# Query-part stores ahead of the heads' traffic, DVE's wait for them at the first context write, maxima turned two units later

## The chip, the cores and the metric

One core of a Trainium2 chip runs the whole program. The metric is the device time of one execution in microseconds (us); lower is better. The engines are PE (TensorE, matrix products), DVE (VectorE), ACT (ScalarE), POOL (GpSimd) and SP (SyncE, which here only issues DMAs).

## The reference

Two adaptive-layernorm blocks over x of 1024 tokens by 512, all float32. The first holds grouped-query attention with rotary embedding and a small feed-forward part, the second a mixer and a gated feed-forward part. What matters here is the attention of the first block:

```python
q = (x @ Wq.T).reshape(b, t, H, DH).transpose(0, 2, 1, 3)      # H = 32, DH = 16
k = (x @ Wk.T).reshape(b, t, HKV, DH).transpose(0, 2, 1, 3)    # HKV = 8, so 4 query heads for each
q = q * cos + _rotate_half(q) * sin
scores = jnp.einsum('bhgtd,bhkd->bhgtk', qg, k) / math.sqrt(DH)
scores = jnp.where(causal, scores, finfo.min)
attn = jax.nn.softmax(scores, axis=-1)
ctx = jnp.einsum('bhgtk,bhkd->bhgtd', attn, v)
```

and the modulation rows `mod = silu(c) @ wmod` of both blocks, most of which are computed in the shade of the attention.

## The kernel before

**Queries in three parts.** Queries and keys are split into three bf16 parts, whose products give float32 accuracy. The first quarter of the queries is split by DVE. The other three are done by POOL in `rope_queries(c)`, c = 1 to 3: seven operations over 128 x 1024 that end in the tile `qparts` and raise `part_q`. SP stores `qparts` to the scratch `q_parts` in DRAM (semaphore `q_out`), from where `load_queries` and `load_keys` bring the rows of each head into the stacks `Qst` and `Kst`. There is one `qparts`, so `rope_queries(c)` first waits for store c - 1 to land. The tiles `qacc`, `qraw` and `qsw` that POOL works in share their memory with `att`, into which DVE writes the contexts; so DVE must see `part_q >= 3` before its first context write.

**POOL's order** is `rope_queries(1)`, `head_v(0)`, `weigh(0)`, `rope_queries(2)`, `weigh(1)`, `rope_queries(3)`, `head_v(1)`, `weigh(2)`, and so on. `weigh(h)` multiplies a piece of the modulation weights `wmr` (1.28 MB, loaded by SP) and sums it into `wsum`.

**A head body.** There are eight key-value heads. `head_body(n)` interleaves three heads. Head n goes through 36 transposed units (`t_unit`: PE scores of 128 keys x 512, ACT exp into `pr`) and nine PV rounds of PE. Head n + 1 gets the rest of its 20 score units (`s_unit`: PE products into bank pair 0/1 or 2/3, DVE maximum over the row into `mxp`), and head n + 2 its first six. A PE score unit waits until DVE has read the unit two slots before it. After head n + 1's last score unit come its maxima: DVE forms `nm`, PE transposes it (`max_turn`, L937), DVE makes three bf16 parts of it (`maxima`, L1699 to L1704), and SP writes them as rows 96 to 98 of `Qst` (`head_dmas`, L736), which `t_unit(n + 1, 0)` needs. PE's `mod_step` is the product of the piece in `wsum`, which DVE copies to `full` (L1708). The maxima use bank 0 and the mod product bank 2, each as one slot in the same order of slots. `ctx_turn` and `ctx_norm` finish head n - 1 in body n, after score unit 7.

The function `body_steps` lays out the order: each piece has a cost, and its step is the transposed unit behind which PE issues it. PE issues pieces in the list's order once the unit count has reached their step; DVE follows the same list without steps. In bodies 1 to 5 the maxima stand behind unit 24, the mod product behind unit 26, the next head's first score unit behind unit 27 and its second behind unit 28. In body 0 maxima and mod stand behind units 23 and 25, in body 6 behind 25 and 27.

**SP's order.** SP issues its DMAs strictly in program order and stops at each wait. After the loads for heads 0 and 1 it goes through `head_dmas(h)` (waits for the maxima of head h, then the row DMAs, the modulation row, and the next `wmr`), then store h + 1 while h < 3, then the loads for head h + 2, which from h = 1 on wait for all of body h - 1's units.

Of the kernel before, what the change touches and what calls it, by code (L numbers as in the profile page):

```python
# [291 lines left out]
def reduce_cost(s):  # L292

    i, _, heads, kh = SUNITS[s]
    return 160 + heads * width(i, kh)
# [14 lines left out]
def ctx_at(n):  # L310

    if n >= NKV - 2:
        return slots_before(NKV) + 2 * (n - (NKV - 2))
    return slots_before(n + 2, "ctx")
# [6 lines left out]
def body_steps(nxt, nxt2, ctx):  # L321


    todo = []
    if nxt:
        for s in range(AHEAD, NS):
            if s == CTX_AT and ctx:
                todo.append(("ctx", -1, None, 1400))
            todo.append(("s", 1, s, reduce_cost(s)))
        todo.append(("max", 1, None, 1600))  # L330
        todo.append(("mod", 1, None, 300))
    elif ctx:
        todo.append(("ctx", -1, None, 1400))
    if nxt2:
        todo += [("s", 2, s, reduce_cost(s)) for s in range(AHEAD)]
    total = sum(x[3] for x in todo)
    out, sofar = [], 0
    for what, d, s, cost in todo:
        step = sofar * NTU // max(total, 24000)
        out.append((max(step, 3) if what == "ctx" else step, what, d, s))  # L340
        sofar += cost
    return out

# [38 lines left out]
def adaln_two_blocks(nc, a, out):  # L382
    banks, pieces, prods = plan()
    with ExitStack() as ctx:
        cursor = [MISC_B]

        def at(name, shape, dt, offset=None):

            if offset is None:
                offset = cursor[0]  # L390
                size = 4 if dt in (F32, F32R) else 2
                for n in shape[1:]:
                    size *= n
                cursor[0] += (size + 31) // 32 * 32
            return nc.alloc_sbuf_tensor_at(name, shape, dt, offset=offset)

        def sem(name):
            return ctx.enter_context(nc.semaphore(name))
# [41 lines left out]
        qparts = at("qparts", [P, 3, T], BF16, WR_B + 40 * 1024)  # L440
# [94 lines left out]
        qscr = nc.dram_tensor("q_parts", (NKV // 2, 3, P, T), BF16, kind="Internal").ap()  # L535
# [23 lines left out]
        q_raw, part_q = sem("later_queries_copied"), sem("later_query_parts_ready")  # L559
        sw_done = sem("later_queries_swapped")  # L560
        kst_ones = sem("key_rows_of_ones_ready")
        q_out = sem("later_query_parts_out")
# [73 lines left out]
        class Chain:  # L636
# [5 lines left out]
            def link(self, ins):  # L642
                ins.then_inc(self.s, 1)
                self.n += 1
                if self.turn is None:
                    self.eng.wait_ge(self.s, self.n)
                else:
                    self.eng.wait_ge(self.s, self.turn * self.per + self.n)
# [18 lines left out]
        Q_ROWS = ((0, 3), (1, 2), (2, 1))  # L667
        K_ROWS = (3, 2, 1)
        assert sum(n for _, n in Q_ROWS) == sum(K_ROWS) == 6

        block = ctx.enter_context(nc.Block())
# [3 lines left out]
        def _(sp):  # L675
# [28 lines left out]
            def load_keys(n, tok_, done):  # L704

                for r0, parts_ in ((0, 3), (3, 2), (5, 1)):
                    sp.dma_start(Kst[DH * r0:DH * (r0 + parts_), n % 3, tok_], kscr[0:parts_, DH * n:DH * n + DH, tok_])\
                        .then_inc(done, 16)

            def load_queries(n, tok_, done):  # L710

                r = G * DH * (n % 2)
                for k, part in enumerate(Q_PARTS):
                    sp.dma_start(Qst[DH * k:DH * k + DH, n % 3, :, tok_],
                                 qscr[n // 2, part, r:r + G * DH, tok_].rearrange("(g d) t -> d g t", d=DH)).then_inc(done, 16)
# [16 lines left out]
            def head_dmas(h):  # L732

                sp.wait_ge(mt_parts, h + 1)
                for q in range(3):
                    sp.dma_start(Qst[KROWS + q:KROWS + q + 1, h % 3, :, :].rearrange("p g t -> p (g t)"),  # L736
                                 mparts[:, q, :]).then_inc(mrow_in, 16)
                sp.wait_ge(s_read, slots_before(h, NS + 1) + 1)
                sp.dma_start(mscr[h * MODW:(h + 1) * MODW].rearrange("(q n) -> q n", n=MODW // 4), full[0:97:32, 0, 0:MODW // 4])\
                    .then_inc(modrow_out, 16)  # L740
                if h < NKV - 1:
                    sp.wait_ge(wsum_ready, h + 1)
                    sp.dma_start(wmr[:, :, :].rearrange("p c n -> p (c n)"), a["wmr"][h + 1]).then_inc(wmr_in, 16)

            for h in range(NKV):
                head_dmas(h)
                if h < 3:
                    sp.wait_ge(part_q, h + 1)
                    sp.dma_start(qscr[h + 1, :, :, :].rearrange("q p t -> p q t"), qparts[:, :, :]).then_inc(q_out, 16)
                if h < NKV - 2:  # L750

                    sp.wait_ge(q_out, 16 * ((h + 2) // 2))
                    if h:
                        sp.wait_ge(t_full, h * NTU)
                    load_keys(h + 2, every, st_in[h + 2])
                    load_queries(h + 2, every, st_in[h + 2])

            sp.wait_ge(modrow_out, 16 * NKV)

# [61 lines left out]
            for k in range(W2_PIECES):  # L821
                n = min(2, HC1 - 2 * k)
# [8 lines left out]
        def _(pe):  # L831
# [153 lines left out]
            def head_body(n, nxt, nxt2, ctx):  # L985


                todo = body_steps(nxt, nxt2, ctx)
                for k in range(NTU):
                    t_unit(n, k)  # L990
                    if k % 4 == 1:
                        if k > 4:
                            pv_round(n, k // 4 - 1)
                        elif n:
                            pv_round(n - 1, ROUNDS - 1)
                    while todo and (todo[0][0] <= k or k == NTU - 1):
                        _, what, d, s = todo.pop(0)
                        if what == "s":
                            if d == 2 and s == 0:
                                pe.wait_ge(st_in[n + 2], 144)  # L1000
                            s_unit(n + d, s)
                        elif what == "max":
                            max_turn(n + d)
                        elif what == "mod":
                            mod_step(n + d)
                        else:
                            ctx_turn(n - 1, ctx_at(n - 1))
# [527 lines left out]
        def _(dve):  # L1535
# [173 lines left out]

            def ctx_norm(n):  # L1710

                for b in range(2):
                    v = ps[:, 2 * b, :].rearrange("p (g i c) -> p g i c", g=G, c=32)
                    dve.wait_ge(s_full, ctx_at(n) + b + 1)
                    link(V.reciprocal(rec[:, b, :, :], v[:, :, :, 16]))
                    V.tensor_tensor(att[:, 4 * b:4 * b + 4, n * G * DH:(n + 1) * G * DH]
                                    .rearrange("p i (g d) -> p g i d", g=G),
                                    v[:, :, :, 0:DH], rec[:, b, :, :].unsqueeze(3).to_broadcast([P, G, 4, DH]),
                                    ALU.mult).then_inc(s_read, 1)

            def head_body(n, nxt, nxt2, ctx):
                for _, what, d, s in body_steps(nxt, nxt2, ctx):
                    if what == "s":
                        s_unit(n + d, s)
                    elif what == "max":
                        maxima(n + d)
                    elif what == "ctx":
                        ctx_norm(n - 1)
# [15 lines left out]
                s_unit(1, s)  # L1744
            swap_queries(3)
            for n in range(NKV - 1):
                if n == 1:
                    dve.wait_ge(part_q, 3)
                head_body(n, True, n < NKV - 2, n > 0)

            dve.wait_ge(ga_in, 16)
            floor_gate(gabc[:, :], gtmp[:, :]).then_inc(ga_ready, 1)
            head_body(NKV - 1, False, False, True)
            ctx_norm(NKV - 1)
            b = filled(dve, "modT")
            link(V.tensor_copy(modc[:, :], ps[:, b, 0:40]))
# [3 lines left out]
            n = 0  # L1760
# [43 lines left out]
            with dve.Fori(0, HC0 // 2) as i:  # L1804
                for j in range(2):
                    for hf in range(2):
                        name = ("up", j, hf)
                        k = prods.before(name, i)
                        s = prods.at[name][0] % 2
# [4 lines left out]
                        c = bass.ds(2 * i + j, 1)  # L1814
# [18 lines left out]
            for t in range(NT + 1):  # L1833
                if t < NT:
                    s = t % 2
# [43 lines left out]
            for kind, y, hf in MIXER:  # L1879
# [13 lines left out]
                elif kind == "fd":  # L1893
                    for m in range(2):
                        n = 4 * y + 2 * hf + m
# [442 lines left out]
```

## Time and profile before

| | |
|---|---|
| three runs | 853.3, 854.83, 856.59 us; median 854.83 |
| the profiled execution | 854.79 us, its span 853.0 us |
| PE busy | 751.9 us (88% of the span), 3710 matmuls |
| DVE, ACT, POOL busy | 477.2, 314.7, 265.9 us |
| mean granted clock of PE | 0.944 |

The span is what the profiler saw, from the first instruction to the last; the run's own time is 1.8 us longer. A granted clock of 1.00 is PE's 2.4 GHz and 0.50 its 1.2 GHz. Busy shares are averages over stages with different limits: the attention heads (about 91 to 383 us) take PE, ACT and DVE together, and the page's share of POOL says nothing on when POOL holds the others up.

### The profile page before, as it was taken

The numbers are of one execution on the slowest core, as the hardware profiler recorded it, in microseconds if no ns is written. First come the engines' busy times: TensorE is split into PE (matmuls) and PEld (weight loads), VectorE is DVE, ScalarE is ACT, GpSimd is POOL, SyncE is SP. The second block draws the span as 40 slices with busy tenths as digits, with TensorE's granted clock in tenths as the row PEclk, the third lists the DMA queues.
The fourth block names the chain that finished last, engine by engine and source line by source line (L and its number), as shares of the span: only waits on it lengthen the run. The fifth ranks groups of instructions, "written<-read, shape, count | busy, mean of one in ns | idle before, by whom it ended". The sixth has DMA issues, their size and how long they took to land.

```text
span 853.0 us, 10154 instructions
## 1 busy us (share of the span) xinstructions
PE 751.9 (88%) x3710; PEld 444.2 (52%) x3710; DVE 477.2 (56%) x720; ACT 314.7 (37%) x528; POOL 265.9 (31%) x219
## 2 busy tenths in 40 slices
PE   5797983999999999879889999797778899997998
PEld 2343331333333333217658888543346688885886
DVE  3768761667776767306845637793687433336310
ACT  4211352566665656761315510244212322332100
POOL 0318547431312303151236513232223122222500
PEclk9997896999999999999989999998779899998999
DMA  9360623061321410212003300110320011111111
GB/s 323 129 122 2 146 65 83 1 146 44 68 84 27 110 64 1 91 38 62 0 27 112 97 1 1 52 41 1 48 63 29 25 50 49 49 39 36 61 62 38
DMA packets 24111, 53.00 MB, mean 62 GB/s; under 512 B 4252, under 2 KB 8100, under 8 KB 23044
## 3 DMA queue, kind: packets, MB, share of 16 engines
q1 hardware_dynamic: 24068, 52.44, 22.1%
q8 instruction: 26, 0.43, 0.2%
q14 instruction: 17, 0.14, 0.1%
HBM read 45.63 MB, written 6.60 MB: 61 GB/s over the span
## 4 chain that ended last, share of the span: by engine, by line
PE 67%; DVE 11%; issue 8%; POOL 8%; ACT 3%; DMA 2%; SPq 1%; ACTq 0%; POOLq 0%; DVEq 0%
PE ps L833 65%; DVE mxp L1688 2%; ACT pr L1374 2%; DVE xnb L1565 1%; DMA rq<-in_mask 1%; POOL wsum L2100 1%; PE ps L850 1%; PE ps L982 1%; POOL qacc L2070 1%; POOL qsw L2069 1%; POOL qacc L2073 1%; POOL qparts L2004 1%; DVE st L1543 1%; DVE arena L1572 1%; DVE dg L1912 1%
## 5 line engine op out<-in xcount | busy, mean ns | idle before, releaser
L833 PE MATMUL ps<-arena 128*128 128x512 f32 (+1 forms) x1416 | 333.6, 397 | 13.0 <-ACT full L1499 5.4
L833 PEld LDWEIGHTS ps<-arena 128*128 128x128 f32 (+1 forms) x1416 | 266.0, 189 | 74.7 <-DVE arena L1575 11.8
L1688 DVE TENSOR_REDUCE mxp<-ps 128x2 f32<-128x1024 f32 (+3 forms) x160 | 173.4, 1115 | 85.6 <-PE ps L833 69.2
L1374 ACT ACTIVATE pr<-ps 128x512 f32<-128x512 f32 x288 | 161.6, 596 | 118.8 <-PE ps L833 117.0
L833 PE MATMUL ps<-Qst,Kst 99*128 99x512 bf16 x288 | 106.1, 391 | 7.1 <-ACT pr L1374 4.2
L833 PE MATMUL ps<-Kst,Qst 96*128 96x512 bf16 (+3 forms) x384 | 102.6, 339 | 6.5 <-DVE mxp L1688 4.8
L833 PE MATMUL ps<-pr,vr 128*32 128x512 f32 x576 | 79.4, 624 | 0.7 <-ACT pr L1374 0.7
L833 PE MATMUL ps<-maskb,identb 128*128 128x128 bf16 (+1 forms) x320 | 75.3, 258 | 0.0
L833 PEld LDWEIGHTS ps<-Kst,Qst 96*128 96x128 bf16 x384 | 36.4, 100 | 73.1 <-DVE mxp L1688 27.5
L833 PEld LDWEIGHTS ps<-Qst,Kst 99*128 99x128 bf16 x288 | 27.3, 98 | 77.0 <-ACT pr L1374 58.4
L2191 POOL TENSOR_TENSOR arena<-raw,arena 128x1024 fp32r<-128x1024 f32 x11 | 26.6, 2418 | 85.8 <-ACT arena L1440 85.8
L2082 POOL COPY vr<-vtok 128x128 f32<-128x128 f32 x8 | 2.5, 308 | 149.6 <-PE ps L833 149.6
L1957 DVE TENSOR_TENSOR xnb<-ps,full 128x512 f32<-128x512 f32 x22 | 15.2, 691 | 54.9 <-PE ps L833 53.0
L1768 DVE TENSOR_TENSOR x<-ps,x 128x512 f32<-128x512 f32 x24 | 16.1, 684 | 48.4 <-PE ps L833 48.4
L2100 POOL TENSOR_TENSOR wsum<-wsum,wmr 128x640 f32<-128x640 f32 (+2 forms) x27 | 37.5, 1389 | 2.3
L833 PEld LDWEIGHTS ps<-maskb,identb 128*128 128x128 bf16 x320 | 32.3, 101 | 10.7 <-issue 4.0
L1501 ACT ACTIVATE arena<-xnb 128x512 f32 (+1 forms) x22 | 13.9, 631 | 48.3 <-DVE xnb L1957 48.3
L833 PE MATMUL ps<-h0T,wq 128*128 128x512 f32 x64 | 31.4, 622 | 0.2 <-ACT wq L1307 0.2
L850 PE MATMUL ps<-ident,xnb 128*128 128x128 f32 x128 | 18.0, 301 | 11.9 <-DVE xnb L1565 11.9
L1959 DVE TENSOR_TENSOR arena<-xnb,arena 128x512 f32 (+1 forms) x22 | 15.2, 692 | 20.0 <-ACT arena L1501 20.0
L982 PE MATMUL ps<-ident,ot 128*128 128x128 f32 x64 | 10.9, 301 | 17.1 <-DVE mxp L1688 16.0
L850 PEld LDWEIGHTS ps<-ident,xnb 128*128 128x128 f32 x128 | 16.4, 157 | 16.2 <-DVE xnb L1565 16.0
(190 smaller groups left out, 809.8 us busy)
## 6 DMA issues: line engine op xcount, KB each, us to landing
wmr<-in_wmr SPq DMA_DIRECT2D x8, 1280.0 KB, 6.4
raw<-in_w SPq DMA_DIRECT2D x16, 512.0 KB, 3.3
Qst<-q_parts SPq DMA_DIRECT2D x42, 128.0 KB
q_parts<-qparts SPq DMA_DIRECT2D x3, 768.0 KB, 8.5
x<-in_x SPq DMA_DIRECT2D x8, 256.0 KB, 5.9
wm<-in_wm SPq DMA_DIRECT2D x4, 512.0 KB, 7.1
raw<-in_up SPq DMA_DIRECT2D x8, 256.0 KB, 2.6
raw<-in_down SPq DMA_DIRECT2D x8, 256.0 KB, 2.7
```

The lines of the kernel that those rows point to most:

```text
L833: return nc.tensor.matmul(outp, lhs, rhs, start=start, stop=stop, skip_group_check=True)
L850: last = nc.tensor.transpose(ps[:, b, t * P:(t + 1) * P], xnb[:, t, c * P:(c + 1) * P], ident[:, :])
L982: last = nc.tensor.transpose(ps[:, 2 * b, tl(g)], ot[:, b, tl(g)], ident[:, :])
L1374: A(pr[:, k % PRING, :], ps[:, 4 + k % 2, :], ACT.Exp, scale=float(DH) ** -0.5).then_inc(exp_done, 1)
L1501: A(gT[0][:, bass.ds(c, 1), tok[hf]].rearrange("p o n -> p (o n)"), xnb[:, s, :], ACT.Copy)\
L1543: chain.tick(V.bn_stats(st[:, t, :], x[:, 4 * hf + t, :]))
L1688: V.tensor_reduce(mxp[:, kh, g0:g0 + heads, i].rearrange("p (b e) -> p b e", e=per), units, AXX, ALU.max)\
L1768: V.tensor_tensor(x[:, t, :], ps[:, b, :], other, ALU.add).then_inc(read_b[b], 1)
L1957: V.tensor_tensor(xnb[:, s, :], ps[:, b, :], full[:, s, :], ALU.mult).then_inc(read_b[b], 1)
L1959: V.tensor_tensor(gT[1][:, bass.ds(c, 1), tok[hf]].rearrange("p o n -> p (o n)"), xnb[:, s, :], gT[0][:, bass.ds(c, 1), tok[hf]].rearrange ...
L2100: ins = nc.gpsimd.tensor_tensor(wsum[:, n0:n1], wsum[:, n0:n1], to, ALU.add)
L2191: nc.gpsimd.tensor_tensor(W13[slot][1].rearrange("p a b c -> p (a b c)"), raw[:, piece_slot(name), :], W13[slot][0].rearrange("p a b c -> ...
```

## The change

The maxima's step in `body_steps` is two higher. The stores of the query parts are a function of their own: store 1 comes ahead of `head_dmas(0)`, stores 2 and 3 come at the end of the turns h = 0 and h = 1 of SP's loop (behind the loads for heads 2 and 3, ahead of `head_dmas(1)` and `head_dmas(2)`). DVE's wait for `part_q >= 3` moves from the start of body 1 to the first line of `ctx_norm(0)`, which in body 1 follows score units 6 and 7. With the new step, maxima and mod product both stand behind unit 26 in bodies 1 to 5, behind 25 in body 0 and behind 27 in body 6; nothing else changes place.

```diff
@@ -337,7 +337,7 @@
     out, sofar = [], 0
     for what, d, s, cost in todo:
         step = sofar * NTU // max(total, 24000)
-        out.append((max(step, 3) if what == "ctx" else step, what, d, s))
+        out.append((max(step, 3) if what == "ctx" else step + 2 * (what == "max"), what, d, s))
         sofar += cost
     return out
@@ -742,11 +742,14 @@
+            def store_queries(c):
+
+                sp.wait_ge(part_q, c)
+                sp.dma_start(qscr[c, :, :, :].rearrange("q p t -> p q t"), qparts[:, :, :]).then_inc(q_out, 16)
+
+            store_queries(1)
             for h in range(NKV):
                 head_dmas(h)
-                if h < 3:
-                    sp.wait_ge(part_q, h + 1)
-                    sp.dma_start(qscr[h + 1, :, :, :].rearrange("q p t -> p q t"), qparts[:, :, :]).then_inc(q_out, 16)
                 if h < NKV - 2:
 
                     sp.wait_ge(q_out, 16 * ((h + 2) // 2))
@@ -754,6 +757,8 @@
                         sp.wait_ge(t_full, h * NTU)
                     load_keys(h + 2, every, st_in[h + 2])
                     load_queries(h + 2, every, st_in[h + 2])
+                if h < 2:
+                    store_queries(h + 2)
@@ -1709,6 +1714,8 @@
             def ctx_norm(n):
 
+                if n == 0:
+                    dve.wait_ge(part_q, 3)
                 for b in range(2):
@@ -1744,8 +1751,6 @@
             for n in range(NKV - 1):
-                if n == 1:
-                    dve.wait_ge(part_q, 3)
                 head_body(n, True, n < NKV - 2, n > 0)
```

## Rows read from the trace of the kernel before

**Rows 1.** The page, its chain of work that ended last, shares by engine.
```profile
PE 67%; DVE 11%; issue 8%; POOL 8%; ACT 3%; DMA 2%; SPq 1%; ACTq 0%; POOLq 0%; DVEq 0%
```

**Rows 2.** Windows: stretch, its length, each engine's busy us (instructions), granted clock, DMA, GB/s.
```profile
147.00:153.00 6.00, 5.74 (x24) 2.49 (x25) 2.69 (x6) 1.19 (x2) 5.50 (x6) 0.50 0.00 0
185.00:191.00 6.00, 5.73 (x40) 2.10 (x41) 4.30 (x8) 3.87 (x8) 5.18 (x10) 1.00 0.92 114
```

**Rows 3.** Timeline of DVE: start, us, operation, [idle before it, and its releaser].
```profile
145.97 2.36 DVE L1688 TENSOR_REDUCE mxp<-ps 128x2 f32<-128x1024 f32 x2 [15.81 <-POOL qparts L2073]
```

**Rows 4.** Timeline of POOL, 60 to 150 us.
```profile
72.77 2.12 POOL L2073 TENSOR_TENSOR qparts<-qacc,qparts 128x1024 bf16<-128x1024 f32 x1
...
95.28 2.34 POOL L2067 TENSOR_TENSOR qacc<-qraw,cosb 128x1024 f32<-128x1024 f32 x1 [11.79 <-DMA q_parts<-qparts]
...
109.16 0.80 POOL L2098 TENSOR_SCALAR wsum<-wmr,sc 128x640 f32<-128x640 f32 x1
...
132.08 2.35 POOL L2067 TENSOR_TENSOR qacc<-qraw,cosb 128x1024 f32<-128x1024 f32 x1 [14.57 <-DMA q_parts<-qparts]
...
143.82 2.12 POOL L2073 TENSOR_TENSOR qparts<-qacc,qparts 128x1024 bf16<-128x1024 f32 x1
```

**Rows 5.** Timeline of SP's DMA issues, 80 to 180 us.
```profile
86.68 0.43 SPq L749 DMA_DIRECT2D q_parts<-qparts  x1
...
122.79 0.38 SPq L749 DMA_DIRECT2D q_parts<-qparts  x1
129.86 1.93 SPq L707 DMA_DIRECT2D Kst<-k_parts  x3
...
172.34 1.87 SPq L736 DMA_DIRECT2D Qst<-mparts  x3
```

**Rows 6.** Timeline of PE: score unit 7 in bodies 1, 2, 3, and body 1's context.
```profile
132.28 0.61 PE L833 MATMUL ps<-Kst,Qst 96*128 96x512 bf16 x2
...
147.25 2.24 PE L982 MATMUL ps<-ident,ot 128*128 128x128 f32 x8 [13.93 <-DVE mxp L1688]
...
183.31 0.60 PE L833 MATMUL ps<-Kst,Qst 96*128 96x512 bf16 x2
...
218.00 0.60 PE L833 MATMUL ps<-Kst,Qst 96*128 96x512 bf16 x2
```

**Rows 7.** Timeline of PE: maxima, mod and next head's unit 1, bodies 0 and 1.
```profile
117.70 0.27 PE L937 MATMUL ps<-ident,nm 128*32 128x128 f32 x1 [2.15 <-DVE nm L1694]
...
121.87 0.42 PE L833 MATMUL ps<-Kst,Qst 96*128 96x256 bf16 x1
...
170.60 0.27 PE L937 MATMUL ps<-ident,nm 128*32 128x128 f32 x1 [1.47 <-DVE nm L1694]
...
172.34 0.48 PE L833 MATMUL ps<-wsum,ones 128*32 128x160 f32 x8
...
173.66 0.27 PE L833 MATMUL ps<-Kst,Qst 96*128 96x256 bf16 x1
```

**Rows 8.** Timeline of DVE: the maxima of heads 0, 1 and 2.
```profile
79.61 1.50 DVE L1702 TENSOR_TENSOR mt<-mt,mparts 32x128 f32<-32x128 f32 x1
...
116.42 1.14 DVE L1694 TENSOR_TENSOR nm<-mxp 128x32 f32<-128x32 f32 x1
...
170.91 0.28 DVE L1699 TENSOR_SCALAR mt<-ps 32x128 f32<-32x128 f32 x1 [0.45 <-PE ps L937]
...
172.88 0.32 DVE L1708 COPY full<-ps 128x160 f32<-128x160 f32 x1 [0.57 <-PE ps L833]
```

**Rows 9.** Timeline of ACT: the exps of units 23 and 24 of body 1.
```profile
168.86 1.09 ACT L1374 ACTIVATE pr<-ps 128x512 f32<-128x512 f32 x2 [0.17 <-PE ps L833]
```

**Rows 10.** DMA issues, 60 to 200 us: count, KB each, median us from issue to landing.
```profile
q_parts<-qparts SPq DMA_DIRECT2D x3, 768.0 KB, 8.5
...
Qst<-mparts SPq DMA_DIRECT2D x9, 8.0 KB, 1.8
```

**Rows 11.** Timeline of PE: the first transposed unit of body 2.
```profile
181.13 0.38 PE L833 MATMUL ps<-Qst,Kst 99*128 99x512 bf16 x1
```

## Prediction before the run

> **What bounds the kernel now.** I read the page's chain of work first, to see whose time the span is made of: 67% of it is PE, but 8% each is POOL and time in which nothing is waited for that the profile shows [rows 1]. A stage in which POOL sets the pace of a PE-bound kernel is the thing to look for. The timelines of DVE, PE and POOL from 60 to 260 us show it once. DVE stands 15.81 us, until 145.97, for the last `qparts` of POOL [rows 3]. That is `part_q >= 3`, which DVE asks for ahead of everything in head body 1. PE, which needs DVE's reads to get its score banks back, stands 13.93 us for it [rows 6].
>
> Then read back why POOL was late. It stood twice for a store of the query parts to land, 11.79 us until 95.28 and 14.57 us until 132.08 [rows 4]. The first store was issued at 86.68, though its data were ready when POOL ended `rope_queries(1)` at 74.89 (72.77 + 2.12): in SP's queue it stood behind `head_dmas(0)`, which waits for the maxima of head 0. The second was issued at 122.79 with data ready at 109.2, behind `head_dmas(1)` [rows 4, 5].
>
> The second thing is small and repeats. In head body 1 PE stands 1.47 us for `nm` before the maxima's transpose, and so in bodies 2 to 5; in body 0 it is 2.15 us [rows 7]. Body 2 to body 3 is exactly 34.69 us (183.31 to 218.00) [rows 6].
>
> **Part 1, the stores.** Nothing is added or removed: the same three stores of 768 KB, the same waits, in another order.
>
> Store 1 is issued at about 74.9. A store took 8.5 us to land when it shared the DMA engines with the 1.28 MB of `wmr` [rows 10]; at that time none is in flight, so 8.5 is an upper bound, and it lands by 83.4. POOL ends `weigh(0)` at 83.49 (95.28 less 11.79), so it no longer waits. `rope_queries` takes 13.86 us (132.08 to 145.94) and `weigh` 8.35 (109.16 to 117.51) [rows 4]. So: `rope_queries(2)` 83.6 to 97.4, `weigh(1)` to 105.8. Store 2 is asked for before `head_dmas(1)`: issued at 97.5, and landed by 106.8 if it takes the 9.3 us that it took from 122.79 to 132.08. `rope_queries(3)` then starts between 105.9 and 106.8 and `part_q` is 3 at 119.8 to 120.7, instead of 145.94.
>
> What stands behind the moved waits on SP: behind store 1, `head_dmas(0)`, which has no work before 83.6; behind store 2, `head_dmas(1)`, whose maxima come at about 119, some 20 us after 97.5; behind store 3, `head_dmas(2)`, while the store itself comes after the loads for head 3 (129.86 [rows 5]) when `part_q` has long been 3. I cost all three at nothing. The loads for head 2 move from 95.23 to about 86.7, under the same body 0, and are used at about 120: nothing.
>
> **Part 2, the wait.** In body 1 DVE now reduces score units 6 and 7 first and asks for `part_q` at the first context write, about 134. It is 13 us early, so no stall at all. The length of the gain is read from body 2, which does the same instructions: PE reaches unit 7 at 132.28 in body 1 and at 183.31 in body 2, 51.03 us; body 2 to body 3 is 34.69. The difference, **16.34 us**, holds the stall and the slow clock behind it: in 147 to 153 PE was granted 0.50 (its 1.2 GHz level) and did 24 matmuls, in 185 to 191, at 1.00 (2.4 GHz), it did 40 [rows 2]. I take that slow stretch as gone with the idle time ahead of it. If it came all the same the part gives about 14.6 (unit 7 to the first work behind the context: 2.6 in body 2, 17.2 in body 1, by the timeline of PE).
>
> The Trainium skill (TensorE: Matmul & The Clock Gate, What's actually happening) has the array fall to the lower level when idle and return after sustained work; the trace agrees, 0.50 behind the 13.93 us.
>
> **Part 3, the maxima two units later.** Only the maxima's transpose moves; the mod product already stood one or two units behind it and now follows it at once, and the first score unit of the next head keeps its place. Body 1: PE passes the old place at 169.13 (170.60 less 1.47) instead of standing. Unit 25 needs the exp of unit 23, which ends at about 169.5 (the first of the pair that starts at 168.86) [rows 9]. Unit 25, the PV round and unit 26 take 1.63 (from 170.71 to 172.34 [rows 7]), so the transpose starts at about 171.12, and `nm`, ended at 170.46 (170.91 less 0.45), is waiting for it: the 1.47 is gone. But DVE's chain hangs on the transpose: transpose 170.60, `mt` at 170.91, four conversions that end at 172.31 (172.88 less 0.57), then the copy of the mod row, 0.32 [rows 7, 8]. Begun at 171.12 it ends at 173.18. Score unit 1 of the next head uses the bank of that copy, and PE could reach it at 172.6; it must now wait until 173.2. Before, it started at 173.66. So of 1.47 only **0.43 to 0.46** is kept, and the wait has moved from `nm` to the copy. For bodies 1 to 5: 5 x 0.43 = **2.15**. Body 6 waited for nothing there: 0.
>
> Body 0 is open. There the old wait was 2.15. `rope_queries(3)` now runs until 119.8 to 120.7, over the maxima of head 1, and DVE's small SBUF operations stretch beside POOL: the subtraction took 1.50 us at 79.61 against 0.28 free, and `nm` 1.14 at 116.42 against 0.19 [rows 8]. Lower bound: chain starts only after POOL ends at 120.7, copy done at 122.2, PE's unit 1 at 122.3 against 121.87 before [rows 7]: minus 0.4. Upper bound: nothing stretches, the whole 2.15 is gained. It is nearer the stretched rows, because POOL is busy there; I take **0.7**.
>
> The Trainium skill (SBUF — State Buffer, Who interferes with whom) says it as an exclusive lock: a DVE operation with two SBUF inputs, or a cast in a two-port mode, blocks for the whole of a GpSimd instruction that came first, and a reduction never does. The 1.50 at 79.61 agrees. It speaks against this change in body 0; by it alone the sum would take 0 there instead of 0.7.
>
> **Sum.** 16.34 + 2.15 + 0.7 = 19.2 us. The profiled execution took 854.79 us (span 853.0); the median of the three runs, 854.83, is the same. Forecast **835.6**. Behind attention everything shifts as a whole: the gate row and its scaling in body 7 come 0.6 later against PE and have more than 5 us of cover ahead of the output projection.
>
> **Rivals.** A: *the maxima's waits go entirely*, because the copy is done earlier than I reckon. For: DVE is idle 0.57 before it now [rows 8]. Against: in the new order it follows the chain. 16.34 + 5 x 1.47 + 2.15 = 25.8, so 829.0; 0.10.
>
> B: *the maxima's move gives nothing* or the slow clock behind body 1's start stays. For: the wait only changes its name, and the slow level came behind a wait of 2.15 too (unit 1 of the next head: 0.42 a matmul at 121.87, 0.27 at 173.66 [rows 7]). 854.8 less 16.3 = 838.5, with the slow clock 840.2, with body 0's loss 840.6; 0.12.
>
> C: *POOL is late anyway*, `part_q` 3 still near 145.9, because something other than the stores holds it. Then DVE has done two reductions (2.36, [rows 3]) and PE some units before they stop: 2.4 to 6, with part 3 846 to 850. Against: both idle rows of POOL name the store; 0.05.
>
> D, on the other side: *the row maxima arrive too late for the next head.* The three row DMAs were issued from 172.34 to 174.21 and land 1.8 later, 176.0; body 2's first unit, which needs them, is at 181.13 [rows 5, 10, 11]. Cover 5.1 us; I shift them by 0.5. To be slower by 4.3 all told, six heads must each lose (19.2 + 4.3)/6 = 3.9, that is, maxima 9.0 us later than now. The stretched rows add 1.2 per operation. It would give 859 and more; 0.03.
>
> The forecast itself, 832.5 to 838.5, has 0.70. With A and B in, 829.5 to 840.5 leaves out no more than 2 in 10. Beyond 0.5% (4.3 us, about what a measurement of this kernel can tell) faster are the forecast, A, B and nearly all of C: 0.95; the rest of C 0.02 the same; D 0.03 slower.
>
> **What would show it.** DVE without a wait for POOL in body 1; POOL's two waits for stores gone, its third `rope_queries` ended at about 120; the first store issued at 75; bodies 1 to 5 each 34.2 to 34.3 us; no PE idle before the transpose but 0.6 before unit 1 of the next head. Wrong if a stall of PE of more than 3 us is left between 120 and 160, or if a body is longer than 34.69.

## The result, and the profile after

| | before | changed |
|---|---|---|
| median of four runs each | 855.71 us (853.3 to 856.6) | 835.05 us (834.61 to 836.39) |
| ratio to before | | 0.9765, 95% interval 0.974 to 0.9791 |
| profiled execution, its span | 854.79, 853.0 us | 836.39, 834.6 us |
| mean granted clock of PE | 0.944 | 0.957 |

The change takes 20.7 us off. The forecast was 835.6. (Lines of the changed file stand 5 higher than before in PE's and DVE's code: the maxima's transpose is L942, its row in [rows 7] L937.)

The page of the changed kernel, its chain of work by engine. POOL had 8% of the chain and "issue" 8% [rows 1]:

```profile
PE 74%; DVE 12%; issue 5%; ACT 4%; POOL 2%; DMA 1%; SPq 1%; ACTq 0%; DVEq 0%; POOLq 0%
```

SP's issues in the changed kernel, 75 to 135 us (the answer to [rows 5]). The stores are L748:

```profile
75.94 0.38 SPq L748 DMA_DIRECT2D q_parts<-qparts  x1
84.69 1.88 SPq L736 DMA_DIRECT2D Qst<-mparts  x3
...
98.43 0.38 SPq L748 DMA_DIRECT2D q_parts<-qparts  x1
...
129.63 1.93 SPq L707 DMA_DIRECT2D Kst<-k_parts  x3
131.61 2.76 SPq L714 DMA_DIRECT2D Qst<-q_parts  x6
134.41 0.96 SPq L748 DMA_DIRECT2D q_parts<-qparts  x1
```

POOL's timeline of the changed kernel: the starts of the second and third `rope_queries` and the last operation of the third. Neither start has a wait any more, where [rows 4] had 11.79 and 14.57 us:

```profile
84.47 2.40 POOL L2072 TENSOR_TENSOR qacc<-qraw,cosb 128x1024 f32<-128x1024 f32 x1
...
106.71 2.36 POOL L2072 TENSOR_TENSOR qacc<-qraw,cosb 128x1024 f32<-128x1024 f32 x1
...
118.49 2.13 POOL L2078 TENSOR_TENSOR qparts<-qacc,qparts 128x1024 bf16<-128x1024 f32 x1
```

`part_q` is 3 at 120.6, and DVE's first context write comes at 134.1. PE's timeline of the changed kernel: body 1's unit 7 and context, then unit 7 of bodies 2 and 3 (the answer to [rows 6]):

```profile
132.05 0.61 PE L838 MATMUL ps<-Kst,Qst 96*128 96x512 bf16 x2
...
133.98 0.65 PE L987 MATMUL ps<-ident,ot 128*128 128x128 f32 x4 [0.42 <-DVE mxp L1693]
...
166.15 0.61 PE L838 MATMUL ps<-Kst,Qst 96*128 96x512 bf16 x2
...
200.25 0.60 PE L838 MATMUL ps<-Kst,Qst 96*128 96x512 bf16 x2
```

Body 1 to body 2 took 51.03 us and takes 34.10; body 2 to body 3 took 34.69 and takes 34.10 as well. Body 1 is now a body like the others: the wait of 13.93 is one of 0.42, which every body has.

PE's timeline around the maxima of the changed kernel, body 0 and then body 1 (the answer to [rows 7]):

```profile
118.18 0.28 PE L942 MATMUL ps<-ident,nm 128*32 128x128 f32 x1
...
121.86 0.28 PE L838 MATMUL ps<-Kst,Qst 96*128 96x256 bf16 x1 [1.98 <-DVE full L1713]
...
152.94 0.39 PE L838 MATMUL ps<-Qst,Kst 99*128 99x512 bf16 x1 [0.38 <-ACT pr L1379]
...
154.49 0.27 PE L942 MATMUL ps<-ident,nm 128*32 128x128 f32 x1
...
156.49 0.28 PE L838 MATMUL ps<-Kst,Qst 96*128 96x256 bf16 x1 [0.31 <-DVE full L1713]
```

The wait of 1.47 for `nm` is gone, and two smaller ones stand in its place: 0.38 for an exp ahead of unit 25, and 0.31 for the copy of the mod row ahead of the next head's unit 1. DVE's timeline of the changed kernel shows the other side, the maxima of head 1 and of head 2 (the answer to [rows 8]):

```profile
118.50 0.28 DVE L1704 TENSOR_SCALAR mt<-ps 32x128 f32<-32x128 f32 x1 [1.18 <-PE ps L942]
118.82 1.88 DVE L1706 CAST mparts<-mt 32x128 bf16<-32x128 f32 x1
...
121.50 0.30 DVE L1713 COPY full<-ps 128x160 f32<-128x160 f32 x1
...
154.80 0.28 DVE L1704 TENSOR_SCALAR mt<-ps 32x128 f32<-32x128 f32 x1 [0.91 <-PE ps L942]
...
156.13 0.30 DVE L1713 COPY full<-ps 128x160 f32<-128x160 f32 x1
```

In body 0 the cast that takes 0.21 elsewhere took 1.88, and ended at 120.70, just behind the last operation of `rope_queries(3)`, which ended at 120.62.

### The profile page after: what moved, and what is told of

It is laid out like the page before. It is cut to its first block, busy times and chain, and to the rows that moved or that the text cites. A ratio compares the mean times of both kernels' runs of the same rounds, so it can differ in the third digit from the quotient of the medians.

```text
span 834.6 us, 10154 instructions
## 1 busy us (share of the span) xinstructions
PE 749.9 (90%) x3710; PEld 447.0 (54%) x3710; DVE 478.6 (57%) x720; ACT 315.8 (38%) x528; POOL 265.5 (32%) x219
## 4 chain that ended last, share of the span: by engine, by line
PE 74%; DVE 12%; issue 5%; ACT 4%; POOL 2%; DMA 1%; SPq 1%; ACTq 0%; DVEq 0%; POOLq 0%
PE ps L838 71%; DVE mxp L1693 3%; ACT pr L1379 2%; PE ps L855 2%; DVE xnb L1570 1%; DMA rq<-in_mask 1%; DVE st L1548 1%; PE ps L987 1%; PE ps L1057 1%; DVE arena L1577 1%; DVE dg L1917 1%; DVE rt L1875 1%; POOL hrs L2213 0%; DVE arena L1580 0%; POOL rs L2038 0%
## 5 line engine op out<-in xcount | busy, mean ns | idle before, releaser
L838 PE MATMUL ps<-Kst,Qst 96*128 96x512 bf16 (+3 forms) x384 | 100.5, 333 | 9.5 <-DVE mxp L1693 5.4
L838 PE MATMUL ps<-pr,vr 128*32 128x512 f32 x576 | 77.1, 607 | 0.7 <-ACT pr L1379 0.7
L855 PE MATMUL ps<-ident,xnb 128*128 128x128 f32 x128 | 21.5, 339 | 13.3 <-DVE xnb L1570 13.3
L855 PEld LDWEIGHTS ps<-ident,xnb 128*128 128x128 f32 x128 | 19.7, 179 | 17.6 <-DVE xnb L1570 17.3
L2038 POOL TENSOR_TENSOR rs<-ve,mh 128x4 f32<-128x4 f32 x8 | 8.1, 1013 | 53.8 <-DVE ve L1558 53.8
```

The lines of the kernel that those rows point to most:

```text
L838: return nc.tensor.matmul(outp, lhs, rhs, start=start, stop=stop, skip_group_check=True)
L855: last = nc.tensor.transpose(ps[:, b, t * P:(t + 1) * P], xnb[:, t, c * P:(c + 1) * P], ident[:, :])
```

## The experiments

Twelve kernels ran in three groups, each group on one chip with its own runs of the kernel before; a ratio is to those. Two of the twelve were the changed kernel again.

### Stores and wait, without the maxima's move

```diff
-        out.append((max(step, 3) if what == "ctx" else step + 2 * (what == "max"), what, d, s))
+        out.append((max(step, 3) if what == "ctx" else step, what, d, s))
```

> The changed kernel with the maxima at their old step (no two units later). Theory (stores free POOL, the maxima's move is a small repeated gain): no stall of DVE in body 1; body 2 to body 3 again 34.69 us with PE idle 1.47 us ahead of each maxima transpose; 16.3 us faster than before, that is 838 to 840. Rival (the maxima's move did nothing of the measured gain): the same time as the changed kernel, 835 to 836. Rival (it did much more than 3 us): 842 or above.

Measured: 839.6 us against 856.06, ratio 0.9798 (0.976 to 0.9836), 16.5 us faster. Unit 7's context transposes come at 137.22, 171.91, 206.60: bodies of 34.69 from body 1 on, and PE stands 1.47 us for `nm` in bodies 1 to 5 again. 842 and above is out; for the other rival, the time of the changed kernel, the intervals of the two ratios overlap (0.976 to 0.9836 here, 0.974 to 0.9791 there), and the traces decide: 34.69 a body here, 34.10 there. The maxima's move adds 3 us on top by the ratios and 4.5 by the medians; the forecast had 2.85.

Body 0 got longer by the stores. From the start of head 1's last reduction to unit 7 of body 1 it took 17.12 us before and 18.00 here (17.96 in the run with the stores alone), since `nm` now falls beside the last operation of `rope_queries(3)`. DVE's and PE's timelines of this kernel:

```profile
118.55 2.00 DVE L1699 TENSOR_TENSOR nm<-mxp 128x32 f32<-128x32 f32 x1
120.70 0.27 PE L942 MATMUL ps<-ident,nm 128*32 128x128 f32 x1 [3.01 <-DVE nm L1699]
```

The wait was 2.15 before. In the changed kernel the same stretch took 16.54, so in body 0 the maxima's move is worth 1.5 beside the stores, and with 5 x 0.59 for the bodies behind it that is 4.4.

### The maxima's move alone

The first hunk of the change, on the kernel before.

> The kernel before with only the maxima two units later. Theory: DVE still stands for POOL until about 146; bodies 2 to 5 take 34.1 us instead of 34.69, since PE's wait of 1.47 becomes one of 0.3 to 0.9 spread over exps and the copy of the mod row; 2.5 to 4.5 us faster, 851 to 853. Rival (no gain by itself): 855 to 856.

Measured: 850.22 us against 856.06, ratio 0.9931 (0.9909 to 0.9953), 5.8 us faster, more than the 2.5 to 4.5 expected. The bodies are 34.10 us, as expected. DVE's timeline of this kernel shows the stall untouched:

```profile
144.16 2.36 DVE L1688 TENSOR_REDUCE mxp<-ps 128x2 f32<-128x1024 f32 x2 [16.83 <-POOL qparts L2073]
```

and its maxima of head 1, with POOL idle for want of a store, are not stretched: 0.21 for the first cast. The bodies account for 2.95. Body 0 gave too, by way of the store: POOL's last `qparts` ended 1.8 us earlier, because store 2 was issued at 122.28 instead of 122.79 and landed 8.0 us later instead of 9.3. Its row in POOL's timeline, to be held against the one at 132.08 in [rows 4]:

```profile
130.26 2.34 POOL L2067 TENSOR_TENSOR qacc<-qraw,cosb 128x1024 f32<-128x1024 f32 x1 [12.45 <-DMA q_parts<-qparts]
```

That is 4.8 of the 5.8, with one trace of each kernel; why the store landed sooner is not shown.

### The stores alone

As the first experiment, and DVE's wait put back at the start of body 1.

```diff
             def ctx_norm(n):
 
-                if n == 0:
-                    dve.wait_ge(part_q, 3)
...
             for n in range(NKV - 1):
+                if n == 1:
+                    dve.wait_ge(part_q, 3)
                 head_body(n, True, n < NKV - 2, n > 0)
```

> Only the stores moved; DVE's wait for part_q >= 3 stays at the start of body 1 and the maxima at their old step. Theory (the stores alone take the stall away): part_q is 3 at about 120, ten us before DVE asks at 130, so the same as the run with stores and moved wait, 838 to 840, within 1 us of it. Rival (the place of the wait carries part of the gain): 841 or above, with DVE waiting for POOL at the start of body 1.

Measured: 839.53 us, ratio 0.9801 (0.9767 to 0.9835), against 839.6 and 0.9798 with the wait moved. DVE's first reduction of body 1 waits for PE, not for POOL:

```profile
133.51 1.23 DVE L1693 TENSOR_REDUCE mxp<-ps 128x2 f32<-128x1024 f32 x1 [1.08 <-PE ps L838]
```

So beside the stores the moved wait is worth nothing that these runs can tell; the stores carry all of the 16.5.

### The wait alone

The last two hunks of the change, on the kernel before.

> Only DVE's wait moved to the first context write; stores and maxima as before. Theory: POOL still stands for both stores and ends at about 146, so DVE stands some 12 us at the context write instead of 15.8 ahead of the body; 2.4 to 6 us faster than before, 850 to 853. Rival (the wait's place is the whole matter): near 839.

Measured: 851.58 us, ratio 0.995 (0.9928 to 0.9971), 4.5 us faster. DVE stood 11.93 us at the context write, as expected. But PE did not stop where I had it stop. PE's timeline of this kernel:

```profile
147.55 1.93 PE L833 MATMUL ps<-pr,vr 128*32 128x512 f32 x8 [10.82 <-POOL vr L2082]
```

PE stood at the first PV round of head 1, for POOL's copy of v (`head_v(1)`), which stands behind `rope_queries(3)` in POOL's program. Two things hung on POOL's lateness and I had named one.

### The wait alone, and the copy of v ahead on POOL

```diff
-            rope_queries(3)
             head_v(1)
+            rope_queries(3)
```

> The kernel before with only DVE's wait moved, and on POOL head_v(1) ahead of rope_queries(3). In the run with only the wait moved PE stood 10.8 us for POOL's copy of v for head 1, which stands behind rope_queries(3) on POOL. Theory (two things hang on rope_queries(3): DVE's write and that copy): PE now runs the PV round and stops for DVE's context read instead, 8 to 11 us, so the time changes by 2 us or less against that run, 850 to 853. Rival (the copy of v was the only thing that held PE): near 840.

Measured: 853.61 us, ratio 0.9972 (0.995 to 0.9994). PE did the PV round and stopped for DVE instead:

```profile
149.23 0.29 PE L833 MATMUL ps<-Kst,Qst 96*128 96x128 bf16 x1 [10.88 <-DVE att L1718]
```

10.88 us where it was 10.82. The second hold was real and freeing it gave nothing: the ratio is 0.002 higher than with the wait alone, at the edge of the 2 us expected, and the two intervals overlap. The changed kernel frees both, since it is POOL that is earlier.

### The changed kernel again, and with the copy of the mod row first

These test what is left of the maxima's wait. The changed kernel on this chip:

> The changed kernel once more, on the chip of the next three, to be their measure: 834.5 to 836.5 and a ratio to before of 0.976.

Measured: 835.82 us, ratio 0.9764 (0.9738 to 0.979).

Then DVE's copy of the mod row, the last of `maxima`, goes ahead of the four conversions, behind the read of the transposed maxima:

```diff
                 V.tensor_scalar(mt[:, 0, :], ps[0:32, 0, 0:P], -1.0, None, ALU.mult).then_inc(s_read, 1)
+                dve.wait_ge(s_full, slots_before(h, NS + 1) + 1)
+                if h:
+                    dve.wait_ge(modrow_out, 16 * h)
+                V.tensor_copy(full[:, 0, 0:MODW // 4], ps[:, 2, 0:MODW // 4]).then_inc(s_read, 1)
                 dve.wait_ge(s_read, slots_before(h, NS) + 1)
                 link(V.tensor_copy(mparts[:, 0, :], mt[:, 0, :]))
...
-                dve.wait_ge(s_full, slots_before(h, NS + 1) + 1)
-                if h:
-                    dve.wait_ge(modrow_out, 16 * h)
-                V.tensor_copy(full[:, 0, 0:MODW // 4], ps[:, 2, 0:MODW // 4]).then_inc(s_read, 1)
```

> The changed kernel, with DVE's copy of the mod row put between its read of the transposed maxima and the four conversions. Theory (PE's new wait ahead of the next head's score unit 1 is for the copy at the chain's end): that wait goes in bodies 1 to 5 (0.3 us each) and in body 0 (1.98 us, there behind a cast that POOL holds up for 1.88); bodies 33.8 us instead of 34.1; in all 2 to 4 us faster than the changed kernel, 831 to 833. Rival (PE is paced by ACT's exps there, the wait only changes its name): bodies stay at 34.1 and only body 0 gains, 833.5 to 835. Rival (row maxima written later for the next head cost): slower than the changed kernel.

Measured: 838.98 us, ratio 0.9799 (0.9772 to 0.9826): 3.2 us slower than the changed kernel, where 2 to 4 faster was expected. The bodies did become 33.62 us (context transposes at 174.05, 207.67, 241.29), 0.48 less each. The loss is ahead of them. DVE's timeline of this kernel at the maxima of head 0:

```profile
85.36 0.32 DVE L1708 COPY full<-ps 128x160 f32<-128x160 f32 x1 [5.14 <-PE ps L838]
85.61 1.11 DVE L1710 CAST mparts<-mt 32x128 bf16<-32x128 f32 x1
86.75 2.45 DVE L1711 TENSOR_TENSOR mt<-mt,mparts 32x128 f32<-32x128 f32 x1
89.24 2.32 DVE L1712 CAST mparts<-mt 32x128 bf16<-32x128 f32 x1
91.59 1.16 DVE L1713 TENSOR_TENSOR mparts<-mt,mparts 32x128 bf16<-32x128 f32 x1
```

For head 0 PE puts a query projection between the transpose and the mod product. The copy waits 5.14 us for it, and the four conversions, now behind the copy, fall under the large operations of `rope_queries(2)`, which the earlier store has just made possible: 7.1 us of conversions, where the same four took 4.3 beside `weigh(0)` in the changed kernel and 1.1 under an idle POOL. Each of the four ends just behind another operation of POOL: 86.72, 89.20, 91.56 and 92.75 against 86.65, 89.06, 91.48 and 92.61. PE stood 5.04 us in all this.

The same with the maxima one unit later instead of two:

> As the run with the copy first, but the maxima one unit later instead of two. Theory: PE comes to the transpose behind unit 25 and its PV round, at about the same time, with nm long ready, so within 1 us of the run with the copy first and two units. Rival (each unit of delay counts): 1 to 3 us apart.

Measured: 839.6 us, ratio 0.9816 (0.9789 to 0.9842); bodies 33.62. Within 1 us as expected: with the copy out of the chain, one unit and two are the same.

And with the maxima at their old step:

> As the run with the copy first, but the maxima at the old step. Theory (two separate waits, one for nm and one for the copy): PE stands 1.47 us for nm again, bodies 34.69, and the copy, which then waits for PE's mod product two units later, holds the conversions up; about 3 us slower than the run with the copy first. Rival: the order on DVE is all that counts, same time.

Measured: 846.08 us, ratio 0.9892 (0.9863 to 0.9922), 7.1 us slower than with two units, where 3 were expected. PE's timeline of this kernel has the old wait back, and its bodies are 34.69 (176.80, 211.49, 246.18):

```profile
160.63 0.27 PE L942 MATMUL ps<-ident,nm 128*32 128x128 f32 x1 [1.47 <-DVE nm L1699]
```

The order on DVE without the two units gives nothing per body. Five bodies at 1.07 are 5.4 of the 7.1. Body 1 is longer still, 36.22 us (140.58 to 176.80): behind its wait of 1.47 PE was granted 0.66 in 160 to 165. With those 1.5 us it comes to 6.9.

### The copy first, from head 1 on, and for head 0 alone

The changed kernel once more, as the measure on this chip:

> The changed kernel once more, as the measure of the three runs beside it: 834.5 to 836.5.

Measured: 833.78 us, ratio 0.9749 (0.9721 to 0.9777).

```diff
+                if h:
+                    copy_mod()
                 dve.wait_ge(s_read, slots_before(h, NS) + 1)
                 link(V.tensor_copy(mparts[:, 0, :], mt[:, 0, :]))
...
+                if not (h):
+                    copy_mod()
```

`copy_mod` holds the two waits and the copy.

> The changed kernel with the copy of the mod row first for heads 1 to 7, and for head 0 last as before. Theory (the loss of the run with the copy first for all heads is head 0 alone, whose four conversions then wait for PE's mod product and fall under rope_queries(2), 7.1 us instead of 5.1 and 5.4 us later; the other heads gain 0.48 a body): bodies 33.62 us, body 0 also 1 to 2 us shorter, 3 to 5 us faster than the changed kernel, 831 to 833. Rival (the loss came from somewhere else, such as the row maxima of all heads): slower than the changed kernel, 837 to 840.

Measured: 831.32 us (830.64 to 832.87), ratio 0.9717 (0.9689 to 0.9744): 2.5 us faster than the changed kernel (833.05 to 835.21), inside the 831 to 833 expected but less than the 3 to 5 that were named with it. Bodies are 33.62 us, so 5 x 0.48 = 2.4 is the whole of it. Body 0 gave nothing. PE's timeline of this kernel:

```profile
119.79 0.27 PE L838 MATMUL ps<-Kst,Qst 96*128 96x256 bf16 x1
...
122.70 0.34 PE L838 MATMUL ps<-Kst,Qst 96*128 96x384 bf16 x1 [1.84 <-DVE mxp L1693]
```

Unit 1 of the next head goes 2 us earlier, but unit 2 waits 1.84 for DVE's reduction of unit 0, which is now what stands behind the cast that POOL holds up (1.90).

With the condition turned round (`h == 0`):

> The changed kernel with the copy first for head 0 alone. Theory: all of the cost and none of the gain: bodies 34.10 us, 5 to 8 us slower than the changed kernel, 840.5 to 844. Rival (head 0 is not the cause): the time of the changed kernel.

Measured: 841.08 us, ratio 0.9847 (0.9814 to 0.988), 7.3 us slower than the changed kernel; bodies 34.1. So head 0 alone is the cost, as expected, and the other heads the gain. By the two other runs (3.2 slower with both, 2.5 faster with the gain alone) the cost would be 5.7; the 1.6 between is not followed.

## Why the prediction was right

**Part 1, the stores: right, step by step.** The execution after runs 1.0 us late against before by then (`rope_queries(1)` ends at 75.92 instead of 74.89). Store 1 went out at 75.94. The first two stores landed in 3.5 and 4.7 us, well under the 8.5 and 9.3 that I allowed, so neither was waited for. POOL went from `weigh(0)` into `rope_queries(2)` without a wait (84.47, forecast 83.6), into `rope_queries(3)` at 106.71 (forecast 105.9 to 106.8), and ended at 120.62 (forecast 119.8 to 120.7). That the later places on SP's queue cost nothing held: the loads for head 3 went at 129.63, against 129.86.

**Part 2: right in size, and for a cause that the stores supply.** 16.34 was forecast for body 1, and 51.03 less 34.69 in the run with stores and wait is just that. The two runs without the maxima's move measured 16.5 in all, though body 0 lost 0.9 in them; the 1.0 between is of the size of the 1.5 of slow clock in one body of the execution before (below), and is not shown further. The run with the stores alone says that the moved wait is no part of it. The slow clock behind the stall is gone as I took it: windows of the changed kernel, PE's granted clock is the seventh group of figures (1.00):

```profile
132.00:138.00 6.00, 5.54 (x41) 2.47 (x38) 3.78 (x8) 3.99 (x8) 5.42 (x6) 1.00 0.98 151
```

against 0.50 in [rows 2]. The Trainium skill (TensorE: Matmul & The Clock Gate, What's actually happening) ties the lower level to an idle array; the two traces agree.

**Part 3: the mechanism right, the size too small.** The wait did move from `nm` to the copy. I kept 0.43 to 0.46 of 1.47 a body and it kept 0.59. The term that was off is the time from unit 25 to the end of the copy: I had 1.62 to the transpose and 2.06 from there to the end of the copy; it is 1.55 (152.94 to 154.49) and 1.94 (to 156.43), since DVE starts the copy before the last conversion has ended. Bodies 1 to 5 gave 2.95 instead of 2.15, and were 34.10 us each instead of the 34.2 to 34.3 that I gave as a sign.

**Body 0: 0.7 forecast, 0.6 measured**, from head 1's last reduction to unit 7 of body 1: 17.12 us (115.16 to 132.28) before, 16.54 (115.51 to 132.05) after. Part of it is luck: the 0.7 was a choice between minus 0.4 and 2.15, and the other two profiled executions of the changed kernel took 15.61 and 16.66 for the same stretch, a gain of 1.5 and 0.5. The old wait of 2.15 for `nm` became one of 1.98 for the copy, because one cast was blocked for 1.88. In the execution with 15.61 head 1's last reduction came 1.35 us later, so that `nm` itself fell beside POOL's last operation (2.01 us, the cast 0.21), and PE waited 0.67 for `nm` and 0.32 for the copy. The Trainium skill (SBUF — State Buffer, Who interferes with whom) calls this an exclusive lock that lasts for the whole GpSimd instruction; the cast that ended 0.08 us behind POOL's operation agrees, and the same cast in the run with the maxima alone, under an idle POOL, took 0.21.

**The sum.** 16.34 + 2.95 + 0.6 = 19.9, with 20.7 between the medians and 18.4 between the two profiled executions. My 19.2 was 1.5 short of the medians. That the time still came out within 0.6 of the forecast is luck in part: I took the 19.2 from 854.79, and the median before, of four runs, is 855.71. Up to body 6 the profiled ones are further apart, 21.0 (contexts of body 6: 325.51 and 304.48). 1.5 of that is the execution before, which ran one body's maxima in slow clock behind its 1.47 us wait; its windows:

```profile
309.00:316.00 7.00, 6.64 (x47) 2.41 (x48) 3.66 (x9) 2.98 (x5) 0.00 (x0) 0.76 0.13 29
```

No body from 1 to 5 does in the three profiled executions of the changed kernel. The run with the copy first at the old step has one such body too, and the two runs with the stores at the old step have none, with the same wait of 1.47 in each body; so this clock is not what the maxima's move adds on top of the stores (body 0 is, as shown above), and how often it comes is not known. From the last contexts of attention (382.29 and 361.10, 21.2 apart) to the end the profiled changed execution loses 2.8 again. 1.2 of that is lost by the time PE transposes `xnb` (405.43 and 385.42); in between its granted clock was 0.74 in 361 to 366, against 1.00 in 382 to 387 before. The rest stays open.

**The rivals.** A (all of the maxima's waits go) fell: it is not reached even with the copy first. B (nothing from the maxima's move, or the slow clock stays) fell by the bodies of 34.10 against 34.69 in the runs without the move, and by the clock of 1.00 behind the start of body 1. C, the case of a late POOL, did not come; but the run with the wait alone shows that I had it wrong in one point, since PE would have been held by the copy of v as well. D (maxima too late for the next head) fell: the row DMAs of head 2 went out at 156.23 and body 2's units were not held.

## What to carry to other kernels

When an engine off the main path is late, ask what its own inputs waited for: here a store that was ready stood in a queue behind an unrelated wait, once for 12 us and once for 14, and moving it gave 16.5 us, while moving the victim's wait gave a quarter of that. Moving a piece later only helps up to the next wait in its chain: with the maxima two units later 1.47 us became 0.69 and a body 0.59 shorter, and the copy ahead of the conversions took another 0.48 off a body, for those heads in which the copy's own input was already there. Small operations of DVE in SBUF are priced by what POOL does at that moment, so an earlier POOL can cost part of what it gains: 0.9 us in body 0 with the stores alone.

## What was not expected of the hardware

A DVE cast of 32 x 128, 0.21 us when POOL is idle, took up to 2.32 us beside POOL's 128 x 1024 operations, and four small conversions together 7.1 us instead of 1.1; reductions and copies out of PSUM beside the same operations kept their times (1.23 and 0.33). A wait of 1.98 us in body 0 of the changed kernel left PE's clock at 1.00, one of 2.15 two units earlier in the kernel before was followed by 0.69 (117 to 122), and there one of five equal waits of 1.47 was followed by 0.76 (309 to 316): short waits of about equal length cost clock in one place and not in another.
